# The first product of a mixture of experts turned round: weights stationary, tokens moving

## The reference

```
h   = layernorm(x)
a   = h @ ctx[e].T            # gate and up are the same product
y   = (silu(a) * a) @ ctx[e].T
x1  = x + tanh(g_x) * y       # with the token's own expert e
h2  = layernorm(x1)
out = x1 + tanh(g_f) * fp8_matmul(h2, weight)   # h2 and weight rounded to e4m3 with one scale each
```

## Time and profile before

| | |
|---|---|
| median of 3 runs | 202.78 us (202.16 to 204.98) |
| profiled execution | 201.43 us, span of its instructions 199.7 us |
| busy, share of the span | PE 72%, DVE 78%, ACT 56%, POOL 41%, weight loads 35% |
| 128-row weight loads, 512-column and other matmuls | 727 and 723 |

### The profile page before, as it was taken

How to read it: one execution, slowest core, us unless ns; L and a number is a source line. 1 busy time by engine, 2 the same in 40 slices (tenths; PEclk the granted TensorE clock), 3 DMA queues, 4 the chain that set the end, 5 groups by cost and what they waited for, 6 DMA issues and landing times.

```text
span 199.7 us, 3062 instructions
## 1 busy us (share of the span) xinstructions
PE 144.3 (72%) x723; PEld 69.7 (35%) x727; DVE 156.3 (78%) x351; ACT 112.7 (56%) x166; POOL 81.8 (41%) x117
## 2 busy tenths in 40 slices
PE   0141939998999797999998999999851266566600
PEld 0110424443555343544444445555420223223200
DVE  2876697798758799899989787776686999998820
ACT  2366596887524854688868534233313987666510
POOL 7158787320312344332386673001110023566670
PEclk9999996999999999999999999999997579999985
DMA  0937998200000222111212210000000002132351
GB/s 6 365 113 198 355 408 264 85 2 0 0 3 0 54 56 53 26 39 43 54 26 53 56 26 0 3 0 2 0 5 0 0 0 105 57 153 113 149 208 59
DMA packets 15440, 15.68 MB, mean 79 GB/s; under 512 B 10816, under 2 KB 11328, under 8 KB 15424
## 3 DMA queue, kind: packets, MB, share of 16 engines
q1 hardware_dynamic: 12576, 7.09, 11.8%
q0 software_dynamic: 2560, 8.39, 11.6%
q10 hardware_dynamic: 288, 0.00, 0.1%
HBM read 8.92 MB, written 4.19 MB: 66 GB/s over the span
## 4 chain that ended last, share of the span: by engine, by line
PE 38%; DVE 33%; issue 11%; POOL 7%; ACT 6%; DMA 1%; DVEq 1%; POOLq 0%
PE four_ps L465 10%; PE four_ps L457 10%; PE four_ps L470 9%; DVE w_hi L1044 3%; DVE hT_hi L1052 3%; PE four_ps L498 3%; POOL x L341 3%; PE four_ps L569 2%; DVE bn L880 2%; DVE zT_lo L866 2%; DVE bn L832 2%; DVE x L1056 2%; ACT y L703 2%; DVE z L861 2%; DVE w_lo L824 2%
## 5 line engine op out<-in xcount | busy, mean ns | idle before, releaser
L364 POOL DMA_INDIRECT out<-x,token_of x16 | 19.3, 1208 | 25.4 <-DVE x L1056 22.9
L359 POOL TENSOR_TENSOR rstd<-var,minus_half 128x1 f32<-128x1 f32 x16 | 8.8, 552 | 49.3 <-DVE var L888 49.3
L633 ACT ACTIVATE zT_hi<-four_ps 128x512 f16<-128x512 f32 x19 | 11.3, 595 | 18.9 <-PE four_ps L498 18.9
L457 PE MATMUL four_ps<-w_hi,hT_hi 128*128 x76 | 21.3, 394 | 0.8 <-ACT w_hi L596 0.7
L624 ACT ACTIVATE sg<-four_ps,job_inv_a 128x512 f32<-128x512 f32 x19 | 12.9, 679 | 15.4 <-PE four_ps L470 12.4
L341 POOL DMA_INDIRECT x<-in_x,token_of x16 | 17.4, 1088 | 7.0 <-issue 4.2
L457 PE MATMUL four_ps<-w_hi,zT_hi 128*128 x76 | 19.5, 379 | 0.8 <-ACT zT_hi L633 0.8
L465 PE MATMUL four_ps<-w_lo,hT_hi 128*128 x76 | 19.9, 384 | 0.0
L615 ACT ACTIVATE w<-x,nmr,rstd 128x512 f32<-128x512 f32 x16 | 13.0, 810 | 11.9 <-DVE nmr L894 11.5
L470 PE MATMUL four_ps<-w_hi,zT_lo 128*128 x76 | 19.5, 379 | 0.0
L465 PE MATMUL four_ps<-w_lo,zT_hi 128*128 x76 | 19.5, 379 | 0.0
(11 more groups left out here) (148 smaller groups left out, 293.4 us busy)
## 6 DMA issues: line engine op xcount, KB each, us to landing
w<-in_ctx_t SPq DMA_DIRECT2D x4, 1024.0 KB, 9.4
wf<-in_wf_t SPq DMA_DIRECT2D x1, 512.0 KB, 15.4
x<-in_x,token_of POOLq DMA_INDIRECT x16, 5.9
out<-x,token_of POOLq DMA_INDIRECT x16, 2.9
hT_hi<-h_row SPq DMA_TRANSPOSE x9, 2.3
hT_lo<-h_row SPq DMA_TRANSPOSE x9, 2.3
ids_s<-in_ids SPq DMA_DIRECT2D x1, 8.0 KB, 2.9
g_s<-in_g_x ACTq DMA_DIRECT2D x1, 0.5 KB, 2.7
```

Source lines behind the costliest of these rows:

```text
L364: pool.indirect_dma_start(out, bass.IndirectOffsetOnAxis(ap=token_of[:, i:i + 1], axis=0), block_of(x1, i), None, bounds_check=T - 1).then ...
L457: pe.matmul(ps, lhs_hi(k), w_block(w_hi, expert, k), start=(k == 0), stop=False)
```

## The change

`up` is turned round. The stationary operand is now a 128 x 128 square of the weights (`w_square`, contraction block k, output block f), and the 128 tokens of `hT` move; a comes out transposed: four column blocks of the PSUM bank, each with 128 output features as partitions and 128 tokens as columns. Each 512-column matmul of `up` becomes four of 128 columns, 48 in place of 12. z is so transposed already: `transpose_z` goes, and with it the order of TensorE is `down(j-1)`, `up(j+1)`. The halves of z are made from z in SBUF, not from PSUM. a has two PSUM banks (`a_even`, and `a_odd` where zT was); z, zT_hi and zT_lo have two buffers, and the waits go by them: z(j) waits for zT_lo(j-2), z_high(j) for y(j-2), `up(j+1)` for z(j-1).

```
+        def w_square(t, e, k, f):
+            return t[:, bass.ds(e * (K * D) + k * D + f * P, P)]
+        def a_of(j):
+            return a_odd if j % 2 else a_even
+        def z_part(t, j):
+            return t[:, j % 2 * D:(j % 2 + 1) * D]
...
             def up(j, tile, expert):
+                first = j < E
                 if j < BY_DMA:
                     pe.wait_ge(hT_hi_done, j + 1)
                 elif j < TILES:
                     pe.wait_ge(hT_landed[j], 32)
-                product(a_ps[:, :], lambda k: chunk(hT_hi, tile, k), lambda k: chunk(hT_lo, tile, k), expert,
-                        lo_ready, j if isinstance(j, int) and j < E else None).then_inc(a_done, 1)
+                if j > 1:
+                    pe.wait_ge(z_done, j - 1)
+                def by_hi(k, w, last=False):
+                    for f in range(K):
+                        mm = pe.matmul(a_of(j)[:, f * P:(f + 1) * P], w_square(w, expert, k, f),
+                                       chunk(hT_hi, tile, k), start=(w is w_hi and k == 0 and f == 0), stop=(last and f == K - 1))
+                    return mm
+                def by_lo(last):
+                    if j < BY_DMA:
+                        pe.wait_ge(hT_lo_done, j + 1)
+                    for k in range(K):
+                        for f in range(K):
+                            mm = pe.matmul(a_of(j)[:, f * P:(f + 1) * P], w_square(w_hi, expert, k, f),
+                                           chunk(hT_lo, tile, k), start=False, stop=(last and k == K - 1 and f == K - 1))
+                    return mm
+                for k in range(K):
+                    if first:
+                        pe.wait_ge(w_hi_done, K * j + k + 1)
+                    by_hi(k, w_hi)
+                if first:
+                    by_lo(False)
+                for k in range(K):
+                    if first:
+                        pe.wait_ge(w_lo_done, K * j + k + 1)
+                    mm = by_hi(k, w_lo, first and k == K - 1)
+                if not first:
+                    mm = by_lo(True)
+                mm.then_inc(a_done, 1)
...
-            def transpose_z(j):
-                pe.wait_ge(z_done, j + 1)
-                for k in range(K):
-                    mm = pe.transpose(zT_ps[:, k * P:(k + 1) * P], z[:, k * P:(k + 1) * P], ident[:, :])
-                mm.then_inc(zT_done, 1)
...
-                transpose_z(j)
                 if not isinstance(j, int) or j + 1 < JOBS:
                     up(j + 1, next_tile, next_expert)
...
-            def zT_high(j):
-                act.wait_ge(zT_done, j + 1)
-                if not isinstance(j, int) or j > 0:
-                    act.wait_ge(y_done, j)
-                act.activation(zT_hi[:, :], zT_ps[:, :], ACT.Copy).then_inc(zT_hi_done, 1)
+            def z_high(j):
+                act.wait_ge(z_done, j + 1)
+                if j > 1:
+                    act.wait_ge(y_done, j - 1)
+                act.activation(z_part(zT_hi_two, j), z_part(z_two, j), ACT.Copy).then_inc(zT_hi_done, 1)
...
             def z_of(j):
                 dve.wait_ge(silu_done, j + 1)
-                if j > 0:
-                    dve.wait_ge(zT_done, j)
-                dve.scalar_tensor_tensor(out=z[:, :], in0=a_ps[:, :], scalar=job_z_mul[:, j:j + 1], in1=sg[:, :],
-                                         op0=ALU.mult, op1=ALU.mult).then_inc(z_done, 1)
+                if j > 1:
+                    dve.wait_ge(zT_lo_done, j - 1)
+                dve.scalar_tensor_tensor(out=z_part(z_two, j), in0=a_of(j), scalar=job_z_mul[:, j:j + 1],
+                                         in1=sg[:, :], op0=ALU.mult, op1=ALU.mult).then_inc(z_done, 1)
+            def z_low(j):
                 dve.wait_ge(zT_hi_done, j + 1)
-                dve.tensor_tensor(zT_lo[:, :], zT_ps[:, :], zT_hi[:, :], ALU.subtract).then_inc(zT_lo_done, 1)
+                dve.tensor_tensor(z_part(zT_lo_two, j), z_part(z_two, j), z_part(zT_hi_two, j), ALU.subtract)\
+                    .then_inc(zT_lo_done, 1)
```

More of the change, by code:

```diff
@@ L143, in gated_experts_kernel @@
         az = sb("az", [P, D], F32)
-        z = sb("z", [P, D], F32)
-        zT_hi = sb("zT_hi", [P, D], F16)
-        zT_lo = sb("zT_lo", [P, D], F16)
+        z_two = sb("z_two", [P, 2 * D], F32)
+        zT_hi_two = sb("zT_hi_two", [P, 2 * D], F16)
+        zT_lo_two = sb("zT_lo_two", [P, 2 * D], F16)
         bn1 = sb("bn1", [P, 6], F32)
@@ L173, in gated_experts_kernel @@
         four_ps = psum("four_ps", [P, 4 * D], F32)
-        a_ps, y_ps, hT_ps, zT_ps = [four_ps[:, n * D:(n + 1) * D] for n in range(4)]
+        a_even, y_ps, hT_ps, a_odd = [four_ps[:, n * D:(n + 1) * D] for n in range(4)]
         r_ps = psum("r_ps", [P, 512], F32)
@@ L207, in gated_experts_kernel @@
         hT_hi_done, hT_lo_done = sem("hT_hi_done"), sem("hT_lo_done")
-        a_done, az_done, silu_done, z_done, zT_done = sem("a_done"), sem("az_done"), sem("silu_done"), sem("z_done"), sem("zT_done")
+        a_done, az_done, silu_done, z_done = sem("a_done"), sem("az_done"), sem("silu_done"), sem("z_done")
         zT_hi_done, zT_lo_done, y_done, x1_done = sem("zT_hi_done"), sem("zT_lo_done"), sem("y_done"), sem("x1_done")
@@ L370, in z_of @@
                 pool.wait_ge(az_done, j)
-                pool.wait_ge(zT_done, j)
-                pool.tensor_tensor(z[:, :], az[:, :], sg[:, :], ALU.mult).then_inc(z_done, 1)
+                if j > 1:
+                    pool.wait_ge(zT_lo_done, j - 1)
+                pool.tensor_tensor(z_part(z_two, j), az[:, :], sg[:, :], ALU.mult).then_inc(z_done, 1)
             def job(j):
@@ L449, in transpose_h @@
                 mm.then_inc(hT_done, 1)
-            def product(ps, lhs_hi, lhs_lo, expert, lo_ready, first=None):
-                for k in range(K):
[L455 to L471, removed]
             def up(j, tile, expert):
+                first = j < E
                 if j < BY_DMA:
@@ L478, in up @@
                     pe.wait_ge(hT_landed[j], 32)
-                def lo_ready():
+                if j > 1:
[6 more added lines that the diff above has]
+                def by_lo(last):
                     if j < BY_DMA:
                         pe.wait_ge(hT_lo_done, j + 1)
-                product(a_ps[:, :], lambda k: chunk(hT_hi, tile, k), lambda k: chunk(hT_lo, tile, k), expert,
-                        lo_ready, j if isinstance(j, int) and j < E else None).then_inc(a_done, 1)
+                    for k in range(K):
[16 more added lines that the diff above has]
+                mm.then_inc(a_done, 1)
             def down(j, expert):
@@ L491, in down @@
                     pe.wait_ge(x1_done, j)
-                product(y_ps[:, :], lambda k: zT_hi[:, k * P:(k + 1) * P], lambda k: zT_lo[:, k * P:(k + 1) * P],
-                        expert, lambda: pe.wait_ge(zT_lo_done, j + 1)).then_inc(y_done, 1)
-            def transpose_z(j):
-                pe.wait_ge(z_done, j + 1)
-                for k in range(K):
-                    mm = pe.transpose(zT_ps[:, k * P:(k + 1) * P], z[:, k * P:(k + 1) * P], ident[:, :])
-                mm.then_inc(zT_done, 1)
+                for t, w in (zT_hi_two, w_hi), (zT_hi_two, w_lo), (zT_lo_two, w_hi):
+                    if t is zT_lo_two:
+                        pe.wait_ge(zT_lo_done, j + 1)
+                    for k in range(K):
+                        mm = pe.matmul(y_ps[:, :], z_part(t, j)[:, k * P:(k + 1) * P], w_block(w, expert, k),
+                                       start=(t is zT_hi_two and w is w_hi and k == 0),
+                                       stop=(t is zT_lo_two and k == K - 1))
+                mm.then_inc(y_done, 1)
             def expert_of(j):
@@ L623, in silu @@
                     act.wait_ge(z_done, j)
-                act.activation(sg[:, :], a_ps[:, :], ACT.Silu, scale=job_inv_a[:, bass.ds(j, 1)]).then_inc(silu_done, 1)
+                act.activation(sg[:, :], a_of(j), ACT.Silu, scale=job_inv_a[:, bass.ds(j, 1)]).then_inc(silu_done, 1)
                 if z_on_pool(j):
-                    act.activation(az[:, :], a_ps[:, :], ACT.Copy, scale=job_z_mul[:, bass.ds(j, 1)])\
+                    act.activation(az[:, :], a_of(j), ACT.Copy, scale=job_z_mul[:, bass.ds(j, 1)])\
                         .then_inc(az_done, 1)
-            def zT_high(j):
-                act.wait_ge(zT_done, j + 1)
-                if not isinstance(j, int) or j > 0:
-                    act.wait_ge(y_done, j)
-                act.activation(zT_hi[:, :], zT_ps[:, :], ACT.Copy).then_inc(zT_hi_done, 1)
+            def z_high(j):
[3 more added lines that the diff above has]
+                act.activation(z_part(zT_hi_two, j), z_part(z_two, j), ACT.Copy).then_inc(zT_hi_done, 1)
             def job(j):
@@ L647, in job @@
                 if not fixed or j < JOBS:
-                    zT_high(j)
+                    z_high(j)
                 for i in [2] if j == 0 else first_in(j):
@@ L858, in z_of @@
                 dve.wait_ge(silu_done, j + 1)
```

(15 more changed lines are left out.)

## The result

The changed kernel takes 232.08 us (231.9 to 232.22, 4 runs) against 202.47 us of the kernel before on the same chip: ratio 1.148, 95% interval 1.143 to 1.153, so 15% slower. The forecast was 226 us in a range of 214 to 252. The profiled execution took 232.19 us, its span is 230.5; span against span it is 30.8 us more.

A forecast was written before the change was run, and what follows sets the result against it. TensorE's sequencer was taken to bound the changed kernel at 7.6 us a job: +23.7 for 15 jobs, +1 ahead, -1.3 behind, 0 tail, sum +23.4 on 201.43, 224.8; with 1.35 to the median, 226 us, range 214 to 252.

The forecast's parts named there:

- The step that decides: In up, 36 address operations make TensorE's sequencer need 4.4 us a job, against 1.5 before.
- Rival C: In up, w_hi addresses are made again for hT_lo, 1.5 us more a job: 249 us; chance 0.10.
- A job: From down(2) to down(17), each job takes the sequencer's 7.6 us, not 6.02: 15 jobs, +23.7 us.
- irregular pauses: Small sequencer pauses that grow with the count; the job's sum of 7.55 us was taken as 7.6.
- The end of the stage: Behind down(17): down(18) can start after 2.6 us, not 3.97, so -1.3 us.
- Ahead of down(2): Start to down(2): three ups longer in the sequencer, up(1) loses its 3.2 us wait; +1, between -3 and +4.
- The tail: From 147 us on: no edit there, so 0.
- A: TensorE's array decides, as addresses are cheaper or the sequencer runs far enough ahead: 196 us; chance 0.10.
- B: In up, weight loads of 98 ns don't hide behind 128 columns; job 7.3 us, 221 us; chance 0.05.
- D: TensorE's clock drops to 1.2 GHz as the array works half the time in up: about 273 us; chance 0.04.
- What the changed profile would show: Signs: 36 to 40 address rows per job in up, period near 7.6 us, array's busy share falling, no wait for z.
- the forecast's two ends: Whole kernel: the forecast's own range without rivals, 214 to 237 us; chance 0.71.

The follow-up runs named there:

- the control: The kernel before, with the first product's addresses written as constants: 203.49 us, ratio 1.003.
- the split from job 4 on: The kernel before with a in two PSUM banks and z's transposes moved inside the next first product, only from job 4 on: 204.25 us, ratio 1.005.
- constants for w_lo: The changed kernel with constant addresses for the squares of w_lo alone: 209.03 us, ratio 1.034 to the kernel before.
- the constants: The changed kernel with all addresses of the first product written as constants of this input: 200.0 us, ratio 0.987 to the kernel before.

## Why the prediction was right, and where its sizes were off

**The step that decides held.** The first product turned round needs 36 new addresses a job, and TensorE's sequencer works them out at 0.11 to 0.16 us each. The counts over the whole span of the changed kernel, which answer to the earlier trace rows:

```profile
L475 PEldq FUSED_REGOPS  x304: 46/46/88, 21.7 to 166.0; - x152
...
L475 PEldq ALU_OP  x304: 32/32/33, 24.4 to 167.9; - x152
...
L484 PEldq ALU_OP  x76: 32/32/42, 23.9 to 168.4; - x76
```

That is 16, 16 and 4 in each of 19 jobs, as forecast; the squares of w_hi stay in registers for the hT_lo group. Rival C (made twice) became a kernel of its own and takes 264 us, where 249 was worked out for it: the sum had 1.5 us a job, measured 1.69, and nothing for the jobs ahead of down(2), measured 6 us.

**A job grew by 1.78 us, not 1.58.** The job of 7.80 us against 7.6 is the largest error: 3 of the 7 us between the span's +30.8 and the forecast's +23.4. The forecast had 0.05 us a job for irregular pauses between address operations. In the job shown, sixteen ALU_OPs and the step to the next line take 135.2 to 137.0, 0.113 each, but the fused ones 2.3 us and not 2.1; the whole sequencer sum by the prices of the earlier trace rows is 7.55. So the pauses are some 0.25 us a job, beside 48 pairs and 36 address operations where there were 12 and 12. What makes them was not tried.

**The end of the stage was forecast at -1.3 and is 0.** The step "down(18) can start after 2.6" looked at the chain a, silu, z, z_high alone. It left out the wait for y's single bank, behind VectorE's 0.75 us of adding: [1.18 <-DVE x L889] above. The run with two banks for y confirms the 2.60 us, but not the gain: down(18) then starts 1.3 us sooner and VectorE's last adding of y no sooner at all. So the term itself was wrong, and not only for the bank: what ends this stretch is VectorE's queue.

**Ahead of down(2)** +2.0, within the -3 to +4 given. The wait of 3.2 us for z before up(1) went as said, but behind it stood one of 1.33 us for hT_hi: up(1) begins at 28.37, only 0.9 us before the 29.23 of the kernel before, and is 5.6 us long where it was 4.3.

**The tail was forecast at 0 and is +2.2** in the profiled execution, though nothing of it changed. It is TensorE's clock. The profile after has a granted clock of 0.84 from 190 to 205 us (the column before the last two; PE's busy time is the first after the length); the kernel before had 0.96 in the same stretch of its tail, 161.5 to 176.5. Below it the same eight matmuls in both kernels, first the changed one:

```profile
190.00:205.00 15.00, 9.64 (x57) 5.04 (x58) 12.74 (x16) 9.71 (x12) 5.76 (x4) 0.84 0.15 60
```

```profile
194.63 3.44 PE L583 MATMUL four_ps<-wf_q,qT 128*128 128x512 bf16 x8
```

```profile
165.87 1.89 PE L569 MATMUL four_ps<-wf_q,qT 128*128 128x512 bf16 x8
```

With 0.53 granted, the lower level (1.2 GHz), the eight take 3.44 us; with 1.00 granted, 2.4 GHz, 1.89. The same code took from 52.2 to 55.2 us in the profiled executions of the runs other than the control. Both forms have short and long ones: 52.2 for the kernel before and 54.6 with the split from job 4 on; 52.3 with constants for w_lo and 55.2 with two banks for y. So the +2.2 need no effect of the change; the 52.2 of the kernel before was the short end of what its own form shows.

**The rivals.** A (the array decides) and the narrow loads (B) fell with the constants: 56 ns a pair. The Trainium skill's 81 ns for such pairs (TensorE: Matmul & The Clock Gate, "Back-to-back issue gap") is not what the run with constants shows: 48 pairs in 2.68 us, 56 ns each. D (the clock): granted 1.00 from down(2) at 52.40 to the end of the expert stage, though narrow matmuls were sent only every 0.11 to 0.13 us in it.

**What the changed profile would show.** Right: address rows, job period, no wait for z, VectorE's share down from 78 to 68%, the clock from down(2) on. Wrong: that the array's busy share would fall and its gaps be put down to issue. It rose, for the reason at the top. Wrong too: that the stretch behind the last down would be as now. And A's price for what a perfect turn could gain, 196, was too good: with constants it is 200.0. The wait for z was not what set the jobs in the middle; behind it stood VectorE's queue at 5.72 us, and the 1.3 us at the end were not there to gain.

**The range.** Its own terms give 215 and 235 for the forecast's two ends, where the text has 214 and 237; the measured 232 lies within either.

**No version here beats the kernel before** with addresses that follow the token ids: the nearest, 202.75, 203.26 and 204.25 us, are not faster.

## What to carry to other kernels

Where operands are addressed at run time, count TensorE's sequencer rows per matmul before making matmuls smaller: the array's time stays nearly the same (2.68 against 2.59 us here), the address operations grow with the number of instructions. In these runs a 512-column matmul (0.216 us) hid one address operation (0.11 to 0.16 us), a 128-column one (0.056 us) did not. And before a wait is paid for, find the one behind it: with all addresses of the first product free, the waits for z that were removed gained 1.3%; a start of the last down 1.3 us sooner gained nothing.

## What the runs showed that was not expected

- A pair of load and matmul of which both addresses are in registers costs the sequencer next to nothing, even though the addresses are dynamic: sixteen such pairs behind four ALU_OPs (137.0 to 137.5) were sent in 0.5 us, while the array needed 0.9.
- 128-column pairs run at 56 ns over 48 in a row, with loads of some 98 ns entirely hidden.
- TensorE's busy share went up by 5 points and the weight loads' by 15 in a kernel that is 15% slower.
- The tail of the same code varies by 3.0 us from one profiled execution to another. In the two profiles set side by side the difference lies in matmuls at the clock's lower level.
